# Two dealing transfers of batch 0 moved from behind the attention loop into steps 28 and 30

## What is computed

```python
x = x + tanh(g_xattn) * attention(layernorm(x), ctx, pos, Wq, Wkv, Wout, bout)
x = x + tanh(g_ffn) * moe(layernorm(x), ...)
```

## Time and profile before

| what | value |
|---|---|
| runs | 379.85, 380.12, 381.43 us; median 380.12 us |
| profiled execution | 379.67 us, its span 377.9 us |
| PE busy | 330.3 us, 87% of the span |
| DVE / ACT / POOL busy | 237.7 / 214.8 / 228.1 us |
| dealing transfers (L523) | 48, 47.1 us of POOL |
| mean granted clock of PE | 0.955 of full speed |

### The profile page before, as it was taken

The page is one execution under the profiler, slowest core; times in us unless marked ns, Lnnn a source line. Parts: engine busy times, 40 slices in busy tenths (PEclk is TensorE's granted clock), DMA queues, the critical chain, the costliest instruction groups (busy, mean ns, idle before and its releaser), DMA issues.

```text
span 377.9 us, 8624 instructions
## 1 busy us (share of the span) xinstructions
PE 330.3 (87%) x2574; PEld 260.8 (69%) x2574; DVE 237.7 (63%) x747; ACT 214.8 (57%) x540; POOL 228.1 (60%) x277
## 2 busy tenths in 40 slices
PE   7879999999999998697763999999999999999900
PEld 5557766666666675465542999999999999999800
DVE  7997788879798889395620455455555555545526
ACT  4795799978897977341320455555555555555400
POOL 8466232214124766777772488788888888888830
PEclk9999999999999999996995899999999999999955
DMA  7699999997203223622335388888888888887689
GB/s 227 198 308 309 310 320 317 322 260 184 66 2 101 70 76 100 205 104 105 111 112 158 82 144 144 132 143 148 145 147 144 147 144 137 145 143 115 70 190 298
DMA packets 63296, 62.21 MB, mean 165 GB/s; under 512 B 6259, under 2 KB 61589, under 8 KB 63253
## 3 DMA queue, kind: packets, MB, share of 16 engines
q1 hardware_dynamic: 48532, 44.60, 41.2%
q0 software_dynamic: 13680, 17.05, 28.6%
q10 hardware_dynamic: 1040, 0.01, 0.2%
HBM read 29.01 MB, written 32.63 MB: 163 GB/s over the span
## 4 chain that ended last, share of the span: by engine, by line
PE 59%; DVE 13%; POOL 10%; DMA 6%; issue 5%; ACT 5%; SPq 1%; POOLq 0%; DVEq 0%
PE psum L1655 17%; PE psum L1637 13%; POOL rows_by_block L523 7%; DVE nmax L945 6%; PE psum L1343 5%; PE psum L1628 5%; PE psum L1646 4%; PE psum L1390 4%; DMA sum<-ob,xs 3%; PE psum L1238 2%; ACT probs L653 2%; DMA w<-sum 2%; PE psum L1361 1%; PE psum L1443 1%; PE psum L1324 1%
## 5 line engine op out<-in xcount | busy, mean ns | idle before, releaser
L574 POOL DMA_INDIRECT sum<-ob,xs x79 | 122.3, 1548 | 39.7 <-DVE ob L1208 29.6
L945 DVE TENSOR_REDUCE nmax<-psum 128x2 f32<-128x512 f32 x128 | 80.4, 684 | 12.7 <-PE psum L1343 11.9
L1655 PE MATMUL psum<-w,hT 88*128 (+1 forms) x316 | 81.5, 380 | 0.0
L653 ACT ACTIVATE probs<-psum 128x512 f32<-128x512 f32 x128 | 69.6, 601 | 11.9 <-PE psum L1361 10.9
L1208 DVE TENSOR_SCALAR ob<-psum,gate 128x256 f32<-128x256 f32 x79 | 38.2, 484 | 49.5 <-PE psum L1655 43.8
L794 ACT ACTIVATE hT<-psum,b1b 88x128 f32<-88x128 f32 x158 | 48.8, 357 | 36.0 <-PE psum L1646 36.0
L1637 PE MATMUL psum<-w,xT 128*128 x316 | 61.9, 319 | 0.3 <-ACT xT L785 0.3
L785 ACT ACTIVATE xT<-psum 128x256 f32<-128x256 f32 x79 | 30.3, 384 | 48.2 <-PE psum L1628 48.2
L1655 PEld LDWEIGHTS psum<-w,hT 88*128 88x128 f32 (+1 forms) x316 | 53.8, 190 | 4.6 <-issue 0.3
L523 POOL DMA_INDIRECT rows_by_block<-Vx,slot x48 | 47.1, 982 | 14.9 <-issue 13.1
L1191 DVE COPY hb<-psum 128x176 f32<-128x176 f32 x79 | 27.0, 341 | 37.6 <-PE psum L1637 37.3
(11 more groups left out here) (202 smaller groups left out, 465.9 us busy)
## 6 DMA issues: line engine op xcount, KB each, us to landing
rows_by_block<-blank SPq DMA_DIRECT2D x1, 10744.0 KB, 38.2
xs<-rows_by_block SPq DMA_DIRECT2D x79, 136.0 KB, 2.6
w<-in_L_ffn_rw_dram SPq DMA_DIRECT2D x2, 2816.0 KB, 22.2
w<-in_L_ffn_rw_dram SPq DMA_DIRECT2D x16, 352.0 KB
sum<-blank SPq DMA_DIRECT2D x3, 1152.0 KB, 13.5
w<-sum SPq DMA_DIRECT2D x12, 256.0 KB, 5.6
sum<-ob,xs POOLq DMA_INDIRECT x79
x_sb<-in_x_dram SPq DMA_DIRECT2D x4, 256.0 KB, 4.5
```

Source lines behind the costliest of these rows:

```text
L574: pool.indirect_dma_start(yd[i], bass.IndirectOffsetOnAxis(ap=xs[b % ROWS_AHEAD][:, X_ID:X_ID + 1].bitcast(U32), axis=0), ob[i][:, :], Non ...
L653: act.activation(probs[g % 2][:, :, n, :], st_bank(g, n)[:, :].rearrange("p (t q) -> p t q", t=TB), ACT.Exp, scale=SCALE).then_inc(exp_ok, 1)
L945: dve.tensor_reduce(nmax[i % 2][:, :, n], S_BANK[(4 * i + n) % SB][:, :].rearrange("p (t k) -> p t k", t=TB), AX.X, ALU.max, negate=True). ...
L1655: ins = pe.matmul(Y_BANK[b % 2][:, 0:D], hT[b % 2][0:rows, c, :], w2[0:rows, bass.ds(expert[b], 1), c, :].rearrange("p a n -> p (a n)"), s ...
```

## The change

One line, the table of the deals of batch 0:

```diff
-            DEALT_AT = {27: (0, 2), 28: (2, 4), 29: (4, 6), 30: (6, 7), 31: (7, 9)}
+            DEALT_AT = {27: (0, 2), 28: (2, 5), 29: (5, 7), 30: (7, 9), 31: (9, 11)}
```

## The result

The changed kernel took 377.31 us in the median of 4 runs (377.14 to 377.64) against 380.65 us (379.85 to 381.43) of the kernel before beside it, 3.3 us less. The ratio of this comparison is 0.9884, 95% interval 0.9847 to 0.9921, a gain of 3.0 to 5.8 us; the quotient of the two medians is 0.9912, within the interval. The forecast was 377.8 us, in a range of 377.0 to 379.5, a gain of 2.3 us or 0.6%. The direction is right, and the time lies in the range; the gain does not fit. The profiled execution took 377.64 us, span 375.9 instead of 377.9.

What follows compares the result with a forecast made beforehand. Bound: the chain through POOL's deals and `rough` of batch 2 to the last deal. 2.53 removed less 0.22 for batch 1's slots, taken as 2.30 us, from the 380.12 median gave 377.8 us, range 377.0 to 379.5.

Steps and rivals of the forecast that it cites:

- Five deals instead of seven ahead of the root: On POOL behind the loop, two fewer deals run before the inverse root of batch 2 (`rough`): 2.53 us removed.
- The wait for the slots of batch 1: On POOL, the first deal of batch 1 must wait for DVE to end its slots, starting 0.22 us late.
- The deals in steps 28 and 30 cost nothing: Added deals fit POOL's idle time before the next maxima: 0.7 us cover in step 28, 0.12 us in step 30.
- `rough` 2.30 us earlier, all of it reaching the last deal: Inverse root of batch 2 on POOL starts at 152.26 instead of 154.56; every later link shifts with it.
- From the profile to the median: The 2.30 us gain, taken from the profiled 379.67 us, was also subtracted from the runs' median of 380.12: 377.8 us.
- PE's wait ahead of L1401: PE's 2.67 us wait before the last pair's transposes; starting 2.30 us earlier still leaves 0.38 us after the preceding matmuls.
- A partial gain: Rival: another bound, such as DVE or PE, takes part; gain 0.8 to 1.9 us, 378.2 to 379.3 us; chance 0.25.
- no effect: Rival: something fixed in time between `rough` and the slots of batch 2 keeps them at 169.95; 380.1 us; chance 0.03.
- The rival on PE's clock: At the expert blocks' start, PE restarts earlier but stays longer at 1.2 GHz; slower, up to 382.2 us; chance 0.04.

Runs made afterwards that it cites:

- the four later series: The kernel before, unchanged, timed again beside its variants on three chips: medians of 381.25 to 383.47 us.
- filler of 10: Kernel before with 10 matmuls of the identity into an unread bank in PE's wait ahead of L1401, no deal moved: 380.16 us against 381.91, ratio 0.9951.
- the second comparison: The changed kernel measured once more against the kernel before: 377.59 us against 382.53 us, ratio 0.9868 (0.9826 to 0.9909).

## Why the prediction was wrong in size and right in kind

- **Five deals instead of seven ahead of the root, 2.53 us:** right. **The wait for the slots of batch 1, 0.22 us:** 0.24.
- **The deals in steps 28 and 30 cost nothing:** right; 0.72 us of idle time left in step 28, and in step 30 the maxima followed the deal 0.10 us after its end. The added deal of step 30 took 0.97 us, not the 1.21 of the deal at 148.28.
- **`rough` 2.30 us earlier, all of it reaching the last deal:** right; 2.41 with 0.12 of a better start, and the last deal 2.49 with the same start.
- **From the profile to the median.** This is the step that failed: "The profiled execution took 379.67 us [...] so it would be 377.37. The median of the runs, 380.12, is 0.45 above the profiled one". I took one execution for all, and the term that I left out of the sum is what PE's wait costs besides its length. The profile of the kernel before was of the rarer kind without a fall of the clock behind that wait; 55 of 69 runs have a mean clock under 0.952, where its own is 0.955. I had four numbers from 379.67 to 381.43 and took their differences for scatter. That 377.31 us came out so near 377.8 is in part luck. I had started from executions without the fall, and the changed kernel, whose wait is down to 0.38 us, is like them; the error is in the time of the kernel before, 380.12 us in my sum and 381.25 to 383.47 us in the medians of the four later series.
- **PE's wait ahead of L1401.** I read its 2.67 us only as a limit, "Free by 0.38 us", and looked for the clock only at the start of the blocks, as a rival on the slow side. The wait cost more than its length: filling it gained 1.9 us with no deal moved (filler of 10, ratio 0.9951), and the fall of the clock behind it cost 1.65 us on the path in the profiles. With the 2.3 to 2.4 us of the path that makes 4.2 to 4.3 us, within the intervals of both comparisons (0.9884 and 0.9868). The two together are not shown to the last tenth: the second comparison's 4.9 us lies above the sum, and some of the rest may be the clock at the start of the blocks, which returned 4.3 us after the restart in the one profile of the changed kernel and 5.8 us after it in the other.
- **The rivals.** A partial gain and no effect did not occur. The rival on PE's clock had the right resource, the wrong place and the wrong sign.

## What to carry to other kernels

A wait of PE in the middle of a critical chain can cost more than its length. Here one of 2.7 us was followed in three of six profiles, and by the mean clocks in most executions, by a stretch at 1.2 GHz, which cost 1.65 us more; when an edit closes such a wait, look at the mean granted clock of many runs, not at one profile. Before forecasting from a profile, check whether its mean clock is that of the other runs. Moving work on an in-order engine pays by what stands behind it: two transfers moved into idle slots gained, while moving only the waiting instruction ahead of them left the engine's own work as the limit, with 0.5 us gained on the path.

## What the runs showed of the hardware

- The same wait of 2.67 to 2.69 us of PE was followed by 2.4 GHz in three profiles of one kernel and by about 3.4 us at 1.2 GHz in three others, beginning within 0.5 us of PE's restart. A wait of 2.85 us was followed by 6.8 us of it. At another wait of 2.1 to 2.7 us, in the same program, the clock fell in 16 of 17 profiles.
- With the wait at 1.4 us a mean clock under 0.952 was rare, 3 of 21 runs.
- The clock also fell within attention in two profiles (at about 135.4 and 137.3 us), in windows of 2 us in which PE was busy for 1.88 us and more; it cost 1.5 us each time.
- PE kept at work until 1.26 us ahead of the first block did not keep the clock: it fell 1.5 us after the restart, and after a wait of 2.74 us 1.1 us after it.
- A deal that starts while DVE's 128x384 multiplication of L1119 runs took 1.21 us (148.28, kernel before); one that had started just ahead of the same instruction in the next batch took the usual 0.96 (168.72, the instruction at 168.80).
